# A gated recurrence with a feed-forward layer woven into it: no feed-forward product ahead of the first candidate of a chunk, and no zero-state products in the very first step

## The chip, the cores and the metric

The kernel runs on one core of one Trainium2 chip. The metric is the time of one execution in microseconds (us), lower is better. Engines are named as in the profile: PE is TensorE's matmul side and PEld its weight load, DVE is VectorE, ACT is ScalarE, POOL is GpSimd, SP is SyncE.

## What is computed

x has 2 sequences of 1024 tokens with 256 features. Two layers follow each other, each added to its input:

```
x = x + mixture(x, cond)       # 4 gated experts and 1 shared branch, each 256 -> 1024 -> 256 with gelu
x = x + recurrence(cond, x)    # over the 1024 tokens, state h of 256 per sequence, h starts at zero:
    z = sigmoid(xz[t] + h @ U_z + vz)
    r = sigmoid(xr[t] + h @ U_r + vr)
    hh = tanh(xh[t] + (r * h) @ U + vh)
    h = (1 - z) * h + z * hh
```

xz, xr and xh are products of x (after the first layer) with W_z, W_r and W; the v terms come from cond alone. The gate of each token and expert is found once in the set-up. The recurrence can't be run in parallel over tokens: each step needs the state of the one before.

## The kernel before, in words

**Chunks and steps.** The 1024 steps are 16 chunks c of 64 steps t. One step s = 64 c + t is one pass of the chain PE, ACT, DVE:

1. Reset gate (R): 12 small products (float16 weights, state split into a high and a low part) add h @ U_r to the PSUM bank `r_ps`, in which the input term already lies. Then ACT takes the tanh, and DVE makes p = r * h (`p_cur`, L633) and its low part `p_low` (L646).
2. Update gate (Z): 8 products after those of R (12 in the first step of a chunk, where the shared form of `recur_two` can't be used). DVE collects `z_sum` (L641, or L639 for t = 0), ACT takes its tanh, DVE makes the two halves of `blend` (L654, L656).
3. Candidate (C): 12 products with p once DVE has it, ACT's tanh, and DVE's scan (L662) makes the new state. `h_low` (L665) and `h_high16` (L666) follow, then two operations that the chain does not need at once: `half_h` (L667) and the output `out_feat` (L672).

The semaphore `preact` counts finished gate sums (three a step); ACT waits for it ahead of the tanh of R and C, DVE ahead of `z_sum`. Every engine works its queue in program order, so what stands ahead of an instruction delays it.

**Side work.** While PE would wait inside a step, it computes the first layer for the next chunk. There are two windows in a step: window 0 lies after the Z products and ahead of the C products, window 1 after the C products and ahead of the next step's R products. The work is a list of 165 units, in the order of `units`: 40 tiles of hidden features, each with two `UP` products (float32, 128 columns, two records each in the trace), ACT's gelu, a scaling by the expert's gate on POOL (L288; tiles of the shared branch have none), and two `DOWN` products three tiles later; 2 `BIAS` units; and one `IDLE` unit for each of the first three tiles, a product without use, 256 columns long in window 0 and 384 in window 1 (`IDLE_FILL`). `SIDE[t, w]` says which units go into which window, and `places` how many: 1 in window 0, 2 in window 1 (one less where a finished block of 16 output steps is transposed, `TURNS`). A window with no unit gets that many idle products instead, and so does every window of chunk 15, which has no next chunk. Ahead of the C products comes one more short idle product (`idle_beside_y`, L690).

**Waits of the side work.** The first `UP` of tile i waits for the gelu of tile i - 2, since the two tiles share a PSUM bank (`if n >= 2: pe.wait_ge(gelu_done, n - 1)`, L738). ACT takes the gelu of a tile in the step t + w, where (t, w) is the window of its second `UP` (`GELU_STEP`), and there behind the candidate's tanh. Two other things are placed from the lists: the seeds of the candidate's bank for the next chunk (`c_seeds`, on DVE at the end of a step without a gelu), and the residual add of step 57 (`RESIDUAL_STEP`, L603), which waits for the last `DOWN`. The input products (`PROJECT`) follow from step 58.

**Start.** Chunk 0 of the first layer is computed before the recurrence. Then come two residual adds on DVE, 12 input products (`project(0, g, m, k)`, L774, g in the order R, Z, C) and step 0. The state is zero there, but all its products are issued.

Of the kernel before, what the change touches and what calls it, by code (L numbers as in the profile page):

```python
# [15 lines left out]
P = 128  # L16
# [23 lines left out]
def moe_gru_kernel(nc, x, cond, gate_w, gate_b, time_w, time_b, ew1, eb1, ew2, eb2, sw1, sb1, sw2, sb2,  # L40
# [4 lines left out]
    KC = D // P  # L45
    CT = TOKENS
    CH = T // CT
    COLS = CT * B
# [38 lines left out]
    UP, DOWN, BIAS, TURN, PROJECT, IDLE = "up", "down", "bias", "turn", "project", "idle"  # L87
    SIDE = {(t, w): [] for t in range(CT) for w in range(2)}
    TURNS = [(t, 1) for t in range(1, CT, STEPS)]
    places = lambda t, w: 1 + w - ((t, w) in TURNS)  # L90
    units = []
    for i in range(BR * HT + LAG):
        if i < BR * HT:
# [35 lines left out]
    with ctx:  # L129
        def sb(name, shape, dt=F32):  # L130
            return ctx.enter_context(nc.sbuf_tensor(name, shape, dt))

        def pb(name):
            return ctx.enter_context(nc.psum_tensor(name, [P, RANK], F32))

        def sem(name):
            return ctx.enter_context(nc.semaphore(name))

        x_rows = sb("x_rows", [P, XT, B, D])
        feat = sb("feat", [P, KC, T * B])  # L140
# [12 lines left out]
        wx = sb("wx", [P, GATES, KC, D])  # L153
# [51 lines left out]
        gate_ps = [pb("r_ps"), pb("z_ps"), pb("c_ps")]  # L205
# [59 lines left out]
        preact = sem("preact")  # L265
# [416 lines left out]
        def _(pe):  # L682
            mm = pe.matmul

            def idle(columns, bank=0, start=False):
                mm(up_ps[bank][:, IDLE_AT:IDLE_AT + columns], ident16[:, :], keep_warm[:, 0:columns],
                   start=start, stop=True, skip_group_check=True)
# [7 lines left out]
            for i in range(XT):  # L695
# [4 lines left out]
                for k in range(KC):  # L700
                    for b in range(B):
                        at = (k * B + b) * P
                        last = pe.transpose(turn_ps[i % 2][:, at:at + P], x_rows[:, i, b, k * P:(k + 1) * P],
                                            ident[:, :])
# [11 lines left out]
            for k in range(KC):  # L716
                mm(y_ps[0:B, 64:64 + 2 * E], silu_v[:, k, :], time_w_sb[:, k, :], start=(k == 0), stop=False,
                   skip_group_check=True)
            mm(y_ps[0:B, 64:64 + 2 * E], ones[0:1, 0:B], bias_row[:, 0:2 * E], start=False, stop=True,
               skip_group_check=True)  # L720
# [11 lines left out]
            def up(c, i, k):  # L732
                e, j = TILES[c][i]
                n = TILE0[c] + i
                if k == 0:
                    if c <= 1 and j == 0:
                        pe.wait_ge(up_in[e], 16)
                    if n >= 2:  # L738
                        pe.wait_ge(gelu_done, n - 1)
                last = mm(up_ps[n % 2][:, 0:COLS], up_w[:, e, k, j * P:(j + 1) * P],  # L740
                          feat[:, k, c * COLS:(c + 1) * COLS], start=(k == 0), stop=(k == KC - 1),
                          skip_group_check=True)
                if k == KC - 1:
                    last.then_inc(up_done, 1)
# [26 lines left out]

            def project(c, g, m, k):
                at = (c % 2) * REGION + m * COLS
                mm(gate_ps[g][:, at:at + COLS], wx[:, g, k, m * P:(m + 1) * P], feat[:, k, c * COLS:(c + 1) * COLS],  # L774
                   start=False, stop=False, skip_group_check=True)

            def turn_body(n):
                pe.wait_ge(body_added, n + 1)
                for k in range(KC):
                    last = pe.transpose(rows_ps[:, k * P:(k + 1) * P], out_feat[:, n % 2, k, :], ident[:, :])  # L780
                last.then_inc(turned, 1)

            first_tiles = len(TILES[0])
            for i in range(first_tiles + FIRST_LAG):
# [4 lines left out]
                if i == 4:  # L789
                    pe.wait_ge(agg_made, 1)  # L790
                    for q in range(3):
                        for k in range(KC):
                            mm(y_ps[0:B, 64 + 2 * E:64 + 3 * E], agg[:, q, k, :], gate_w_sb[:, q, k, :], start=False,
                               stop=False, skip_group_check=True)
                    mm(y_ps[0:B, 64 + 2 * E:64 + 3 * E], ones[0:1, 0:B], bias_row[:, 2 * E:3 * E], start=False,
                       stop=True, skip_group_check=True).then_inc(logits_made, 1)
# [5 lines left out]
                if i == FIRST_LAG:  # L802
                    pe.wait_ge(spread_made, 1)
                    mm(y_ps[:, 0:BR * B], ones[0:B, :], spread[:, :, :].rearrange("q e b -> q (e b)"),
                       start=True, stop=True, skip_group_check=True)
                    mm(y_ps[0:BR, 16:16 + B], picked[:, :], ident[0:B, 0:B], start=False, stop=True,
                       skip_group_check=True).then_inc(weights_shared, 1)
# [6 lines left out]
                if i == FIRST_LAG + 8:  # L814
# [3 lines left out]
                    for g in range(GATES):  # L818
                        last = mm(gate_ps[g][:, :], keep_warm[:, 0:P], keep_warm[:, :], start=True, stop=True,
                                  skip_group_check=True)  # L820
# [5 lines left out]
            for k in range(KC):  # L826
                pe.wait_ge(feat_ready, k + 1)
                for g in range(GATES):
                    for m in range(KC):
                        project(0, g, m, k)  # L830
            pe.wait_ge(u_split, GATES)

            HIGH_PRODUCTS = [(m, k, w) for m in range(KC) for k in range(KC) for w in (u_high, u_mid)]
# [3 lines left out]
            def load(g, product):  # L837
                m, k, w = product
                pe.ldweights(w[:, g, k, m * P:(m + 1) * P])  # L839
# [36 lines left out]
            def side(c, t, window):  # L876
                for what, *of in SIDE[t, window]:
                    if what == TURN:
                        n = c * BODIES + t // STEPS
                        if n > 0:  # L880

                            pe.wait_ge(blended, (c * CT + t + 1) * BLEND_STEP + 2)
                            if n > 1:
                                pe.wait_ge(turned_copied, n - 1)
                            turn_body(n - 1)
                    elif what == IDLE:
                        if c < CH - 1:

                            idle(IDLE_FILL[window], (TILE0[c + 1] + of[0]) % 2)
                    elif c < CH - 1:  # L890
                        i, k = of[0], of[1]
                        if what == UP:
                            up(c + 1, i, k)
                        elif what == DOWN:
                            down(c + 1, i, k)
                        elif what == BIAS:
                            output_bias(c + 1, k)
                        else:
                            g, m, k = of
                            if m == 0 and k == 0:  # L900
                                pe.wait_ge(feat_ready, (c + 2) * KC)
                                pe.wait_ge(seeded, (c + 2) * GATES * KC)
                            if g == Z and k == 0:

                                pe.wait_ge(part_ready, (c * CT + t + 1) * PARTS_STEP + Z_CLEAR)
                            project(c + 1, g, m, k)

                real = 0 if c == CH - 1 else sum(what != TURN for what, *_ in SIDE[t, window])
                turning = (t, window) in TURNS
                if real == 0 or c == CH - 1:  # L910
                    for _ in range(1 + window - turning):
                        idle(IDLE_FILL[window])

            for s in range(T):
                c, t = divmod(s, CT)
                parts = s * PARTS_STEP
                load(R, HIGH_PRODUCTS[0])
                pe.wait_ge(part_ready, parts + H_HIGH)
                recur(s, R, False, HIGH_PRODUCTS[0], loaded=True)
                for product in HIGH_PRODUCTS[1:]:  # L920
                    recur(s, R, False, product)
                load(R, LOW_PRODUCTS[0])
                pe.wait_ge(part_ready, parts + H_LOW)
                recur(s, R, True, LOW_PRODUCTS[0], loaded=True)
                for product in LOW_PRODUCTS[1:]:
                    last = recur(s, R, True, product, product is LOW_PRODUCTS[-1])
                last.then_inc(preact, 1)
                for product in MID_PRODUCTS:
                    recur(s, Z, False, product)
                if t == 0:  # L930
                    for product in LOW_PRODUCTS:
                        recur(s, Z, False, product)
                    for product in LOW_PRODUCTS:
                        last = recur(s, Z, True, product, product is LOW_PRODUCTS[-1])
                else:
                    pe.wait_ge(part_ready, parts + H_HIGH16)
                    for product in LOW_PRODUCTS:
                        last = recur_two(s, product, product is LOW_PRODUCTS[-1])
                last.then_inc(preact, 1)
                side(c, t, 0)  # L940
                if t != RESIDUAL_STEP:
                    idle_beside_y(IDLE_SHORT)
                load(C, HIGH_PRODUCTS[0])
                pe.wait_ge(part_ready, parts + PARTS_STEP + P_HIGH)
                recur(s, C, False, HIGH_PRODUCTS[0], loaded=True)
                for product in HIGH_PRODUCTS[1:]:
                    recur(s, C, False, product)
                load(C, LOW_PRODUCTS[0])
                pe.wait_ge(part_ready, parts + PARTS_STEP + P_LOW)
                recur(s, C, True, LOW_PRODUCTS[0], loaded=True)  # L950
                for product in LOW_PRODUCTS[1:]:
                    last = recur(s, C, True, product, product is LOW_PRODUCTS[-1])
                last.then_inc(preact, 1)
                side(c, t, 1)
# [30 lines left out]
```

## Time and profile before

| | |
|---|---|
| median of 3 runs | 1881.32 us (1879.59, 1881.32, 1881.68) |
| profiled execution | 1878.24 us, span in the trace 1876.4 us |
| busy share of the span | PE 98%, PEld 91%, DVE 78%, ACT 38%, POOL 11% |
| mean granted clock of TensorE | 0.999 of full speed |
| chain that ended last | PE 94%, DVE 2%, ACT 2%, issue 1% |

The busy share is the time with an instruction of the engine in flight, so PE at 98% is not PE at its peak: overlapped products and idle products count too. The chain that ended last is followed back through the releases of semaphores; where an engine worked at something else while it waited, the chain stays on that engine.

### The profile page before, as it was taken

How to read it: one execution, taken by the hardware profiler on the slowest of the kernel's cores; microseconds unless marked ns; L12 is line 12 of the kernel's file. 1: busy time of each engine (PE TensorE's matmuls, PEld its weight loads, DVE VectorE, ACT ScalarE, POOL GpSimd, SP SyncE). 2: the span in 40 equal slices, each digit the busy share in tenths (PEclk: the TensorE clock that was granted, in tenths of full speed). 3: DMA queues.
4: the chain of work that ended last, by engine and by line, in shares of the span. 5: the costliest groups of instructions: out<-in, count | busy, mean ns of one | idle time of the engine just before them, and what ended most of it. 6: DMA issues, size and time to landing. Idle time of an engine off the chain costs nothing.

```text
span 1876.4 us, 101766 instructions
## 1 busy us (share of the span) xinstructions
PE 1844.4 (98%) x39969; PEld 1703.9 (91%) x39970; DVE 1454.8 (78%) x11505; ACT 713.4 (38%) x3785; POOL 199.4 (11%) x515
## 2 busy tenths in 40 slices
PE   8999999999999999999999999999999999999998
PEld 8998999989899998999989999899999989999766
DVE  5787878778787787877878787787877878788776
ACT  4333433434333343433434344343433434334322
POOL 0110101101020110101101011110101101011000
PEclk9999999999999999999999999999999999999999
DMA  9000000000000000000000000000000000000000
GB/s 321 4 4 5 5 4 5 5 4 5 5 5 5 4 5 5 4 5 5 4 5 5 4 5 5 4 5 5 4 5 5 4 5 5 5 5 4 5 5 4
DMA packets 16926, 23.62 MB, mean 13 GB/s; under 512 B 3585, under 2 KB 15160, under 8 KB 16445
## 3 DMA queue, kind: packets, MB, share of 16 engines
q1 hardware_dynamic: 15280, 17.05, 2.6%
q8 instruction: 312, 5.11, 1.1%
q14 instruction: 170, 1.38, 0.2%
q10 hardware_dynamic: 1164, 0.07, 0.0%
HBM read 15.01 MB, written 2.10 MB: 9 GB/s over the span
## 4 chain that ended last, share of the span: by engine, by line
PE 94%; DVE 2%; ACT 2%; issue 1%; ACTq 0%; DVEq 0%
PE up_ps L740 20%; PE y_ps L758 20%; PE r_ps L863 13%; PE c_ps L863 13%; PE r_ps L842 6%; PE z_ps L863 6%; PE c_ps L842 5%; PE z_ps L872 4%; ACT rc_tanh_ps L408 2%; PE y_ps L690 2%; DVE h_cur L662 1%; PE c_ps L774 1%; PE z_ps L774 1%; DVE p_cur L633 1%; PE r_ps L774 1%
## 5 line engine op out<-in xcount | busy, mean ns | idle before, releaser
L740 PE MATMUL up_ps<-feat,up_w 128*128 128x128 f32 x2528 | 519.2, 302 | 0.2
L758 PE MATMUL y_ps<-hidden,down_w 128*128 128x128 f32 x2528 | 515.4, 301 | 0.0
L839 PEld LDWEIGHTS <-u_high 128*128 128x128 f16 x4096 | 398.2, 97 | 20.7
L408 ACT ACTIVATE rc_tanh_ps<-r_ps 128x4 f32<-128x4 f32 x1024 | 161.8, 158 | 574.5 <-PE r_ps L863 574.4
L740 PEld LDWEIGHTS up_ps<-feat,up_w 128*128 128x128 f32 x2528 | 362.3, 190 | 1.2 <-ACT hidden L397 0.9
L758 PEld LDWEIGHTS y_ps<-hidden,down_w 128*128 128x128 f32 x2528 | 360.4, 190 | 0.0
L863 PEld LDWEIGHTS r_ps<-h_cur,u_mid 128*128 128x128 f16 x4096 | 252.1, 96 | 113.6 <-issue 46.6
L863 PE MATMUL c_ps<-p_cur,u_mid 128*128 128x40 bf16 (+10 forms) x4096 | 337.4, 179 | 0.0
L863 PE MATMUL r_ps<-h_cur,u_mid 128*128 128x20 bf16 (+5 forms) x4096 | 336.4, 178 | 0.0
L662 DVE TENSOR_TENSOR_SCAN h_cur<-rc_tanh_ps,blend 128x8 f32<-128x8 f32 x1024 | 178.0, 174 | 165.5 <-ACT rc_tanh_ps L408 165.4
L288 POOL TENSOR_TENSOR hidden<-hidden,expert_w 128x128 f32<-128x128 f32 (+3 forms) x416 | 163.9, 394 | 1339.0 <-ACT hidden L397 1339.0
L408 ACT ACTIVATE z_tanh_ps<-z_sum 128x4 f32<-128x4 f32 x1024 | 181.6, 177 | 309.4 <-DVE z_sum L641 304.0
L863 PE MATMUL c_ps<-p_cur,u_high 128*128 128x40 bf16 (+6 forms) x3072 | 285.5, 179 | 0.0
L863 PE MATMUL r_ps<-h_cur,u_high 128*128 128x20 bf16 (+3 forms) x3072 | 285.0, 178 | 0.0
L633 DVE SCALAR_TENSOR_TENSOR p_cur<-rc_tanh_ps,h_cur 128x4 f32<-128x4 f32 x1024 | 166.2, 162 | 138.2 <-ACT rc_tanh_ps L408 126.8
L667 DVE TENSOR_SCALAR half_h<-h_cur 128x4 f32<-128x4 f32 x1024 | 271.9, 266 | 0.0
L863 PEld LDWEIGHTS c_ps<-p_cur,u_mid 128*128 128x128 f16 x4096 | 252.3, 96 | 20.9 <-issue 20.8
L863 PE MATMUL z_ps<-h_cur,u_mid 128*128 128x20 bf16 (+5 forms) x4096 | 259.4, 178 | 0.0
L408 ACT ACTIVATE rc_tanh_ps<-c_ps 128x4 f32<-128x4 f32 x1024 | 161.8, 158 | 252.2 <-PE c_ps L863 252.2
L872 PE MATMUL z_ps<-h_two,u_high 128*128 128x20 f16 x4032 | 240.9, 169 | 0.0
L397 ACT ACTIVATE hidden<-up_ps,small_cols 128x128 f32<-128x128 f32 x632 | 231.6, 367 | 14.5 <-PE up_ps L740 13.2
L672 DVE SCALAR_TENSOR_TENSOR out_feat<-h_cur,h_unscale,feat 128x4 f32<-128x4 f32 x1024 | 223.2, 218 | 0.0
(154 smaller groups left out, 4059.0 us busy)
## 6 DMA issues: line engine op xcount, KB each, us to landing
up_w<-in_L_cond_ew SPq DMA_DIRECT2D x4, 1024.0 KB, 9.3
down_w<-in_L_cond_ew SPq DMA_DIRECT2D x4, 1024.0 KB, 10.4
x_rows<-in_x SPq DMA_DIRECT2D x8, 256.0 KB, 4.6
out<-out_rows SPq DMA_DIRECT2D x128, 16.0 KB, 1.8
up_w<-in_L_cond_sw SPq DMA_DIRECT2D x1, 1024.0 KB, 12.7
down_w<-in_L_cond_sw SPq DMA_DIRECT2D x1, 1024.0 KB, 13.4
cf<-in_L_cond_C_r SPq DMA_DIRECT2D x1, 256.0 KB, 9.6
cf<-in_L_cond_C_z SPq DMA_DIRECT2D x1, 256.0 KB, 9.4
```

What stands on the lines that cost most here:

```text
L397: act.activation(hidden[:, n % TILES_HELD, :], up_ps[n % 2][:, 0:COLS], ACT.Gelu_apprx_tanh, bias=small_cols[:, at:at + 1]).then_inc(gelu_ ...
L408: act.activation((tanh_r, tanh_z, c_now)[g].rearrange("p (m b) -> p m b", b=B), before_tanh, ACT.Tanh, scale=0.5 / GAIN).then_inc(act_done, 1)
L633: dve.scalar_tensor_tensor(p_cur[:, :, 0:B], sq(tanh_r), 1.0, sq(h_now), ALU.add, ALU.mult).then_inc(part_ready, 1)
L662: dve.tensor_tensor_scan(h_cur[:, 0, :], cand, blend[:, :], 0.0, ALU.mult, ALU.add).then_inc(part_ready, 1)
L667: dve.tensor_scalar(half_h[:, :], h_now, -0.5, None, ALU.mult).then_inc(blended, 1)
L672: last = dve.scalar_tensor_tensor(out_feat[:, body % 2, :, row * B:(row + 1) * B], sq(h_now), h_unscale[:, :], feat[:, :, s * B:(s + 1) * ...
L740: last = mm(up_ps[n % 2][:, 0:COLS], up_w[:, e, k, j * P:(j + 1) * P], feat[:, k, c * COLS:(c + 1) * COLS], start=(k == 0), stop=(k == KC ...
L758: last = mm(y_ps[:, m * COLS:(m + 1) * COLS], down_w[:, e, j, m * P:(m + 1) * P], hidden[:, n % TILES_HELD, :], start=False, stop=(m == KC ...
L839: pe.ldweights(w[:, g, k, m * P:(m + 1) * P])
L842: return pe.add_instruction(mybir.InstMatmult(name=nc.get_next_instruction_name(), engine=mybir.EngineType.PE, ins=[pe.lower_ap(moving), p ...
L863: return mm(gate_ps[g][:, at:at + width], w[:, g, k, m * P:(m + 1) * P], moving, start=False, stop=last_of_sum, skip_group_check=True)
L872: return mm(gate_ps[Z][:, at:at + width], w[:, Z, k, m * P:(m + 1) * P], h_two[:, 0:width // B, k * B:(k + 1) * B], start=False, stop=last ...
```

## The change

Three edits. The first takes the one place of window (0, 0) away, so that all 165 units move on by one place and each chunk's first step has an idle product of 256 columns in its window 0. The second and third go together: in step 0 of the whole run no R, Z or C product is issued, only the two windows' side work (without the short idle product), and the last input product of each gate counts `preact` up in their stead. The lists of gelu steps and seeds are derived from `SIDE` and change with it.

```
-    places = lambda t, w: 1 + w - ((t, w) in TURNS)
+    places = lambda t, w: 0 if (t, w) == (0, 0) else 1 + w - ((t, w) in TURNS)
...
             def project(c, g, m, k):
                 at = (c % 2) * REGION + m * COLS
-                mm(gate_ps[g][:, at:at + COLS], wx[:, g, k, m * P:(m + 1) * P], feat[:, k, c * COLS:(c + 1) * COLS],
-                   start=False, stop=False, skip_group_check=True)
+                return mm(gate_ps[g][:, at:at + COLS], wx[:, g, k, m * P:(m + 1) * P],
+                          feat[:, k, c * COLS:(c + 1) * COLS], start=False, stop=False, skip_group_check=True)
...
                 for g in range(GATES):
                     for m in range(KC):
-                        project(0, g, m, k)
+                        last = project(0, g, m, k)
+                    if k == KC - 1:
+
+                        last.then_inc(preact, 1)
...
             for s in range(T):
                 c, t = divmod(s, CT)
                 parts = s * PARTS_STEP
+                if s == 0:
+
+                    side(c, t, 0)
+                    side(c, t, 1)
+                    continue
                 load(R, HIGH_PRODUCTS[0])
```

The lists that follow from it, worked out from the code (U is UP, D is DOWN, I is IDLE, B is BIAS, each with its tile and half; a bar parts window 0 from window 1):

```
step   before                          gelu    after                           gelu
0      U0.0 | I0 U0.1                          (idle) | U0.0 I0
1      U1.0 | I1 TURN                  0       U0.1 | U1.0 TURN                0
2      U1.1 | U2.0 I2                  1       I1 | U1.1 U2.0
3      U2.1 | U3.0 U3.1                2       I2 | U2.1 U3.0                  1
4      B0 | B1 D0.0                    3       U3.1 | B0 B1                    2, 3
5      D0.1 | U4.0 U4.1                        D0.0 | D0.1 U4.0
56     D39.1 | (idle)                          D39.0 | D39.1
seeds of the candidate's bank ahead of steps 24 and 28, after the change ahead of 38 and 42;
residual add at step 57 in both
```

## Rows read from the trace of the kernel before

**Rows 1.** Timeline, DVE: scans around two chunk starts (start us, us, engine, line, operation).
```profile
165.76 0.17 DVE L662 TENSOR_TENSOR_SCAN h_cur<-rc_tanh_ps,blend 128x8 f32<-128x8 f32 x1 [0.17 <-ACT rc_tanh_ps L408]
...
167.60 0.17 DVE L662 TENSOR_TENSOR_SCAN h_cur<-rc_tanh_ps,blend 128x8 f32<-128x8 f32 x1 [0.21 <-ACT rc_tanh_ps L408]
...
169.38 0.17 DVE L662 TENSOR_TENSOR_SCAN h_cur<-rc_tanh_ps,blend 128x8 f32<-128x8 f32 x1 [0.17 <-ACT rc_tanh_ps L408]
...
1758.27 0.17 DVE L662 TENSOR_TENSOR_SCAN h_cur<-rc_tanh_ps,blend 128x8 f32<-128x8 f32 x1 [0.17 <-ACT rc_tanh_ps L408]
...
1760.05 0.17 DVE L662 TENSOR_TENSOR_SCAN h_cur<-rc_tanh_ps,blend 128x8 f32<-128x8 f32 x1
```

**Rows 2.** Timeline, PEld and PE: window 0 of chunk 1's first step.
```profile
166.56 0.30 PEld L740 LDWEIGHTS up_ps<-feat,up_w 128*128 128x128 f32 x2
...
166.89 0.21 PE L690 MATMUL y_ps<-keep_warm,ident 128*128 128x96 bf16 x1
```

**Rows 3.** Timeline: input products and the very first step, three engines.
```profile
51.41 0.61 PE L774 MATMUL z_ps<-feat,wx 128*128 128x128 f32 x4
...
51.86 0.61 PE L774 MATMUL c_ps<-feat,wx 128*128 128x128 f32 x4
...
52.81 0.24 PE L863 MATMUL z_ps<-h_two,u_high 128*128 128x20 f16 x4
...
53.57 0.15 DVE L656 SCALAR_TENSOR_TENSOR blend<-z_tanh_ps,half_h 128x4 f32<-128x4 f32 x1
...
53.74 0.16 ACT L408 ACTIVATE rc_tanh_ps<-c_ps 128x4 f32<-128x4 f32 x1 [0.28 <-PE c_ps L863]
...
53.93 0.17 DVE L662 TENSOR_TENSOR_SCAN h_cur<-rc_tanh_ps,blend 128x8 f32<-128x8 f32 x1 [0.20 <-ACT rc_tanh_ps L408]
```

**Rows 4.** Timeline, ACT and PE: chunk 1, gelu of step 3, first product of step 4.
```profile
172.80 0.37 ACT L397 ACTIVATE hidden<-up_ps,small_cols 128x128 f32<-128x128 f32 x1
...
173.15 0.18 PE L842 MATMUL r_ps<-h_cur,u_high 128*128 128x20 bf16 x1
```

**Rows 5.** Timeline, ACT and PEld, before the recurrence: a gelu waited for, two gelus running.
```profile
17.82 0.37 ACT L397 ACTIVATE hidden<-up_ps,small_cols 128x128 f32<-128x128 f32 x1 [0.77 <-PE up_ps L740]
...
18.24 0.19 PEld L740 LDWEIGHTS up_ps<-feat,up_w 128*128 128x128 f32 x1 [0.20 <-ACT hidden L397]
...
21.46 0.63 ACT L397 ACTIVATE hidden<-up_ps,small_cols 128x128 f32<-128x128 f32 x2
```

**Rows 6.** Timeline, POOL and DVE: one scaling (chunk 1, step 2), two running (chunk 4, step 12).
```profile
169.70 0.40 POOL L288 TENSOR_TENSOR hidden<-hidden,expert_w 128x128 f32<-128x128 f32 x1 [38.72 <-ACT hidden L397]
...
170.27 0.16 DVE L633 SCALAR_TENSOR_TENSOR p_cur<-rc_tanh_ps,h_cur 128x4 f32<-128x4 f32 x1
...
529.51 0.26 POOL L288 TENSOR_TENSOR hidden<-hidden,expert_w 128x42 f32<-128x42 f32 x1 [1.37 <-ACT hidden L397]
...
529.55 0.24 DVE L667 TENSOR_SCALAR half_h<-h_cur 128x4 f32<-128x4 f32 x1
...
529.71 0.37 DVE L672 SCALAR_TENSOR_TENSOR out_feat<-h_cur,h_unscale,feat 128x4 f32<-128x4 f32 x1
...
529.73 0.33 POOL L288 TENSOR_TENSOR hidden<-hidden,nothing 128x86 f32<-128x86 f32 x1
```

**Rows 7.** Timeline, PE and DVE: chunk 1, window 1 of step 55 and the first residual add.
```profile
264.87 0.69 PE L758 MATMUL y_ps<-hidden,down_w 128*128 128x128 f32 x4
...
267.57 0.28 DVE L603 TENSOR_TENSOR feat<-y_ps,feat 128x128 f32<-128x128 f32 x1
```

**Rows 8.** Windows: us, PE, PEld, DVE, ACT, POOL busy (x), granted clock, DMA share, GB/s.
```profile
280.30:283.70 3.40, 3.40 (x58) 3.21 (x55) 1.92 (x17) 0.67 (x5) 0.00 (x0) 0.50 0.00 0
...
1760.00:1870.00 110.00, 99.03 (x2236) 73.89 (x2234) 78.49 (x682) 31.66 (x190) 0.00 (x0) 1.00 0.02 4
```

**Rows 9.** Timeline, DVE: scans of steps 127 and 129, across the start of chunk 2.
```profile
279.44 0.17 DVE L662 TENSOR_TENSOR_SCAN h_cur<-rc_tanh_ps,blend 128x8 f32<-128x8 f32 x1 [0.17 <-ACT rc_tanh_ps L408]
...
284.08 0.17 DVE L662 TENSOR_TENSOR_SCAN h_cur<-rc_tanh_ps,blend 128x8 f32<-128x8 f32 x1 [0.59 <-ACT rc_tanh_ps L408]
```

## The prediction

> **What bounds the kernel now.** I read the busy shares first. PE at 98% looks like the bound, and the chain that ended last agrees, but both count side work and idle products as PE time, so they can't tell a full queue from a filled wait. The timeline can. The scan (L662) ends a step, so the distance of two scans is the step's length. In chunk 1 the scans of steps 63, 64 and 65 start at 165.76, 167.60 and 169.38 [rows 1]: the chunk's first step takes 1.84 us, the next 1.78 us. In chunk 15, whose windows hold nothing but idle products, the first step takes 1760.05 - 1758.27 = 1.78 us too [rows 1]. The 63 steps between scan 64 (167.60) and scan 127 (279.44) average 1.775 us [rows 1, 9], with every mix of UP, DOWN, transposes, seeds and residual adds in them, so a step with float32 units is no longer than one with idle products. What sets its length is the chain from product to tanh to vector operation and back; side work is free as long as it leaves PE, ACT and DVE at the moment when the chain wants them. So the question for each moved unit is what is late behind it.
>
> **The change part by part.**
>
> *The first step of a chunk.* There the Z gate has 12 products instead of 8. The UP unit behind them begins its weight load at 166.56, and the short idle product starts only at 166.89 [rows 2], 0.33 us for one unit, so the candidate's products come late. With an idle product there, as in chunk 15, the step takes 1.78 instead of 1.84 us [rows 1]. I take 0.07 us, since the starts are rounded and the difference lies between 0.05 and 0.08. Chunks 1 to 14 gain it (15 has it already, 0 is counted next): 14 x 0.07 = **-1.0 us**, bounds -0.7 and -1.1.
>
> *The very first step.* The last input products of Z and C end at 51.41 + 0.61 = 52.02 and 51.86 + 0.61 = 52.47 [rows 3]. From then on only ACT and DVE work. Through Z: before, the Z products end at 52.81 + 0.24 = 53.05 and `blend` at 53.57 + 0.15 = 53.72 [rows 3], 0.67 us later, so `blend` is ready at 52.69. Through C: the tanh starts 0.05 us after the products (the release in rows 5), at 52.52, and the scan 53.93 - 53.74 = 0.19 us after the tanh's start [rows 3], at 52.71. Both meet; I take 52.72. The scan moves from 53.93 to 52.72, **-1.2 us**. PE is ready just in time: the input products follow each other at 51.86 - 51.41 = 0.45 us for four records [rows 3], so PE is free for the windows at 52.31; 640 idle columns at 2.4 GHz are 0.27 us and a unit 0.33 us [rows 2], which makes 52.91, and the scan ends at 52.72 + 0.17 = 52.89 [rows 3]. Bounds: -1.0 if PE's windows end last, -1.25.
>
> *A wait in step 3.* Before, the first UP of tile 3 stands in window 1 of step 3 and the gelu of tile 1, for which it waits, in step 2. After the change the UP is still in window 1 of step 3, but the second UP of tile 1 has moved from window (2, 0) to (2, 1), so the gelu of tile 1 moves to step 3, behind that step's candidate tanh. Of all 40 tiles it is the only pair that falls into one step, once in each of chunks 0 to 14. The time of a gelu in step 3 is in the trace: it runs from 172.80 to 173.17, and the next R product comes at 173.15 [rows 4]. PE is released 0.05 us behind a gelu (17.82 + 0.37 = 18.19, weight load at 18.24) [rows 5], at 173.22, and what follows the unit starts 0.33 us after its weight load [rows 2], at 173.55. The R products of step 4 are late by 173.55 - 173.15 = 0.40 us, and nothing but the state's chain stands behind them: they are the chain. 15 x 0.40 = **+6.0 us**. Lower bound: 0.30 a chunk (4.5) if the weight load slips ahead of the wait; upper 0.45 (6.7).
>
> *Two gelus in step 4.* The gelus of tiles 2 and 3 now both stand in step 4. Two running take 0.63 us together [rows 5]; from the usual start, 172.80 [rows 4], they would end at 173.43. The next scan-to-`p_cur` distance of 0.89 us (below) and the 0.19 us from a tanh to the DVE operation behind it put ACT's next tanh at about 173.6, so ACT costs nothing. But both tiles belong to an expert, and POOL scales them one after the other. The first scaling starts 169.70 - 169.38 = 0.32 us behind the scan and takes 0.40 us [rows 1, 6]. Running scalings overlap by 0.04 us (529.51 + 0.26 against 529.73) [rows 6], so the second lasts from 0.68 to 1.08 us behind the scan of step 4. In chunk 4, step 12, a scaling in two pieces shows what DVE does meanwhile: `half_h` ends at 529.79, 0.02 us after the first piece, and `out_feat` at 530.08, 0.02 us after the second [rows 6]. They are held until POOL is done. There the pieces were short enough. With two full ones `out_feat` ends at 1.10, and the operation behind it in DVE's queue, `p_cur`, starts 0.08 us before that (as 529.71 against 529.79) [rows 6], at 1.02 instead of 170.27 - 169.38 = 0.89 [rows 1, 6]. The candidate's products wait for `p_cur`. So 0.13 us a chunk, 15 x 0.13 = **+1.9 us**. Bounds: 0 if `out_feat` gets in between the two scalings; 15 x 0.21 = 3.2 without that overlap.
>
> *What costs nothing.* The last DOWN moves from window 0 to window 1 of step 56. Two such units in step 55 end at 264.87 + 0.69 = 265.56; a step of 1.78 later that is 267.34, and the residual add starts at 267.57 [rows 7]. Cover 0.23 us; gone, each us would go to DVE and the next `p_cur`. The candidate's seeds move to other steps of the same kind, with no gelu in front. All other units only change windows, among steps that average 1.775 us whatever they hold [rows 1, 9]. The added counts on `preact` queue behind nothing.
>
> **Sum:** -1.0 - 1.2 + 6.0 + 1.9 = **+5.7 us**. On the profiled execution 1878.24 gives 1883.9. The median of the runs shown is 3.1 us above that execution, 0.16%, for reasons that no trace here shows; part of it may be the clock (below). Added to the median: 1881.3 + 5.7 = 1887.0 us, 0.30% slower.
>
> **The clock.** From 280.30 to 283.70 the granted clock is 0.50 of full speed (1.2 of 2.4 GHz) [rows 8]. Before it PE had gone through steps 62 and 63 with idle products alone, and stood at the start of chunk 2. From scan 127 to scan 129 it took 284.08 - 279.44 = 4.64 us [rows 9], against 1.84 + 1.78 = 3.62: one such stretch costs 1.0 us. But chunk 15, idle products throughout and PE busy 99.03 of 110 us, ran at clock 1.00 [rows 8]. The change leaves PE less to do at just these places, in the first window and beside the wait in step 3. The Trainium skill (TensorE: Matmul & The Clock Gate, "What's actually happening") says that activity releases the throttle and its lack brings it back, which speaks against thinning PE out at a chunk's start. By that rule alone a fall at every one of the 15 chunk starts would add 14 x 1.0 = 14 us; by the rows of chunk 15 nothing. I put 0 into the sum, nearer to 109 us of rows than to one event, and up to 3 us into the range.
>
> **Rivals.**
>
> *A, both waits (the forecast):* +5.7, 1887.0.
>
> *B, the wait in step 3 alone:* `out_feat` slips between the two scalings. For it: DVE issues it before POOL's second starts. Against: in chunk 4 it was issued before the second piece too (529.71 against 529.73) and still held. +3.8, 1885.1.
>
> *C, not slower:* the wait in step 3 costs nothing, because the gelu is done when PE comes to it. It decides at the point where PE must start the unit to be out by 173.15, that is 172.82 in the times of rows 4; the gelu would have to end by 172.77 and it ends at 173.17. Only if ACT took it ahead of the candidate's tanh would it hold; the queue says otherwise. Then -2.2 + 1.9 = -0.3 (1881.0), and -2.2 (1879.1) if the scalings cost nothing either.
>
> *D, the clock falls more often:* three to fourteen more stretches at 1.0 us over A, 1890 to 1901. For it the one event and its place; against it chunk 15.
>
> That the first edit doesn't do what it says (the candidate still late because of the idle product put in the unit's place) is excluded by chunk 15, where just this product stands there.
>
> **How the numbers follow.** Chances: A 0.63, B 0.17, C 0.08, D 0.12. What a measurement of this kernel can tell from no change is about 0.2%, 3.8 us. A is slower by more than that over nearly all of its bounds (its lower end 4.5 + 1.9 - 2.2 = 4.2); B lies on the line and is split; C is the same; D is slower. That gives slower 0.80, same 0.17, faster 0.03, the last for a median that moves with the clock. The range goes from B with a little less wait, 1884.0, to A with three more stretches at half clock, 1889.8.
>
> **What would show it.** Scans at each chunk start 1.78 us apart; the first scan near 52.7; in the list of waits PEld L740 waiting for ACT's gelu (L397) 15 times inside the recurrence, about 0.3 us each, and the R products behind it 0.4 us late; in step 5 `out_feat` held to 1.10 us behind the scan and `p_cur` at 1.02; a page otherwise unchanged. Wrong would be: no such wait, scans of steps 3 to 6 all at 1.78 us, or a granted clock of 0.50 at many chunk starts.

## The result and the profile after

| | before | changed |
|---|---|---|
| median of 8 runs each, same chip | 1881.07 us | 1886.05 us |
| lowest, highest | 1879.59, 1882.28 | 1885.32, 1890.21 |
| profiled execution, span | 1878.24, 1876.4 us | 1887.49, 1885.7 us |

The ratio is 1.0030, with a 95% interval of 1.0021 to 1.0039: the change makes the kernel slower by 5.0 us. Forecast were 5.7 us, 1887.0 us and a range of 1884.0 to 1889.8. The changed kernel run again on another chip (`e0_changed_again`, below) came out 6.2 us slower.

The busy shares of the changed kernel's page say nothing of it; they are those of before within one point:

```profile
PE 1849.4 (98%) x39918; PEld 1707.2 (91%) x39918; DVE 1449.7 (77%) x11505; ACT 713.0 (38%) x3785; POOL 197.8 (10%) x515
```

The timeline of DVE with the scans alone (start us, us) shows it. These are steps 63 to 70, the counterpart of [rows 1]:

```profile
167.89 0.17 DVE L662 TENSOR_TENSOR_SCAN h_cur<-rc_tanh_ps,blend 128x8 f32<-128x8 f32 x1 [0.17 <-ACT rc_tanh_ps L408]
...
169.67 0.17 DVE L662 TENSOR_TENSOR_SCAN h_cur<-rc_tanh_ps,blend 128x8 f32<-128x8 f32 x1
...
173.22 0.17 DVE L662 TENSOR_TENSOR_SCAN h_cur<-rc_tanh_ps,blend 128x8 f32<-128x8 f32 x1 [0.17 <-ACT rc_tanh_ps L408]
...
175.00 0.17 DVE L662 TENSOR_TENSOR_SCAN h_cur<-rc_tanh_ps,blend 128x8 f32<-128x8 f32 x1 [0.18 <-ACT rc_tanh_ps L408]
...
177.17 0.17 DVE L662 TENSOR_TENSOR_SCAN h_cur<-rc_tanh_ps,blend 128x8 f32<-128x8 f32 x1 [0.17 <-ACT rc_tanh_ps L408]
...
179.06 0.17 DVE L662 TENSOR_TENSOR_SCAN h_cur<-rc_tanh_ps,blend 128x8 f32<-128x8 f32 x1 [0.18 <-ACT rc_tanh_ps L408]
...
180.84 0.17 DVE L662 TENSOR_TENSOR_SCAN h_cur<-rc_tanh_ps,blend 128x8 f32<-128x8 f32 x1 [0.17 <-ACT rc_tanh_ps L408]
```

The first step of the chunk now takes 169.67 - 167.89 = 1.78 us instead of 1.84. Steps 1 to 3 are plain. The scan of step 4 comes 177.17 - 175.00 = 2.17 us behind that of step 3, the scan of step 5 another 179.06 - 177.17 = 1.89 us later, and from there on steps are plain again. Chunks 0 to 14 all show the same: step 4 between 2.172 and 2.177 us, step 5 between 1.886 and 1.891, plain steps 1.776.

**The wait in step 3.** Timeline of ACT, PEld and PE of the changed kernel, and under it the row of its waits (us in total, times, longest):

```profile
174.88 0.37 ACT L397 ACTIVATE hidden<-up_ps,small_cols 128x128 f32<-128x128 f32 x1
...
175.30 0.30 PEld L740 LDWEIGHTS up_ps<-feat,up_w 128*128 128x128 f32 x2 [0.39 <-ACT hidden L397]
175.51 0.10 PEld L842 LDWEIGHTS <-u_high 128*128 128x128 f16 x1
...
175.62 0.18 PE L845 MATMUL r_ps<-h_cur,u_high 128*128 128x20 bf16 x1
```

```profile
PEld up_ps L740 <- ACT hidden L397: 6.4, 18, 0.4
```

The gelu ends at 174.88 + 0.37 = 175.25, the weight load of tile 3's first UP starts 0.05 us later, and the next step's R products 0.32 us behind that. Of the eighteen waits for a gelu three lie in the set-up ([rows 5] show such a one) and fifteen in the recurrence. The weight loads stood idle 0.39 us ahead of this unit (the prediction had said about 0.3).

**The held operation in step 5.** The same step on ACT, POOL and DVE; x2 are two instructions running:

```profile
177.05 0.62 ACT L397 ACTIVATE hidden<-up_ps,small_cols 128x128 f32<-128x128 f32 x2
...
177.50 0.76 POOL L288 TENSOR_TENSOR hidden<-hidden,expert_w 128x128 f32<-128x128 f32 x2 [1.77 <-ACT hidden L397]
...
177.53 0.38 DVE L667 TENSOR_SCALAR half_h<-h_cur 128x4 f32<-128x4 f32 x1
177.84 0.44 DVE L672 SCALAR_TENSOR_TENSOR out_feat<-h_cur,h_unscale,feat 128x4 f32<-128x4 f32 x1
...
178.19 0.15 DVE L633 SCALAR_TENSOR_TENSOR p_cur<-rc_tanh_ps,h_cur 128x4 f32<-128x4 f32 x1
```

The two scalings end at 178.26. `out_feat` takes 0.44 us instead of 0.21 and ends at 178.28; `p_cur` starts 178.19 - 177.17 = 1.02 us behind the scan, against 0.89 in [rows 6].

**The very first step.** Timeline of PE and DVE, the counterpart of [rows 3]:

```profile
54.54 0.61 PE L774 MATMUL c_ps<-feat,wx 128*128 128x128 f32 x4
...
55.23 0.15 DVE L656 SCALAR_TENSOR_TENSOR blend<-z_tanh_ps,half_h 128x4 f32<-128x4 f32 x1
...
55.48 0.17 DVE L662 TENSOR_TENSOR_SCAN h_cur<-rc_tanh_ps,blend 128x8 f32<-128x8 f32 x1
```

From the last candidate input products to the scan it is 55.48 - 54.54 = 0.94 us, before 53.93 - 51.86 = 2.07: 1.13 us gained. That all of it starts later than before comes from the set-up, ahead of the changed code. Windows of the changed kernel's set-up (columns as in [rows 8], the granted clock third from last) show

```profile
7.00:21.00 14.00, 13.32 (x111) 10.60 (x109) 7.68 (x27) 10.59 (x21) 0.00 (x0) 1.00 1.06 379
21.00:31.00 10.00, 10.00 (x62) 9.72 (x62) 7.37 (x38) 3.45 (x9) 0.39 (x1) 0.66 1.06 401
31.00:49.00 18.00, 18.00 (x161) 17.73 (x160) 10.49 (x32) 7.83 (x21) 0.00 (x0) 1.00 0.66 241
...
1424.80:1428.20 3.40, 3.40 (x59) 3.05 (x55) 1.91 (x17) 0.69 (x6) 0.00 (x0) 0.50 0.00 0
```

a stretch at 1.2 GHz between 21 and 31 us, in code that the change does not touch and though PE had been busy 13.32 of the 14 us before it, and one more stretch at half clock at a chunk start, as before had one. `e8_wait_alone_in_before` and `e9_pair_alone_in_before`, which hold none of the three edits, have such a stretch in the set-up too. So the difference of the two spans, 9.3 us, is not the change's price. It is made up of: set-up later by 2.7 (first input product at 52.24, before 49.56), first step -1.1, 14 chunk starts -1.0, waits 15 x 0.398 = +6.0, held operations 15 x 0.111 = +1.7, stretches at half clock -0.1, and 1024 plain steps longer by 1.1 ns each, +1.1. That is 9.3. The change's own parts sum to +5.6 (+5.5 with unrounded terms), against 5.0 measured over the medians.

### The profile page after: what moved, and what is told of

Its sections match the earlier page's. It is cut to its first block, busy times and chain, and to the rows that moved or that the text cites. A ratio compares the mean times of both kernels' runs of the same rounds, so it can differ in the third digit from the quotient of the medians.

```text
span 1885.7 us, 101663 instructions
## 1 busy us (share of the span) xinstructions
PE 1849.4 (98%) x39918; PEld 1707.2 (91%) x39918; DVE 1449.7 (77%) x11505; ACT 713.0 (38%) x3785; POOL 197.8 (10%) x515
## 4 chain that ended last, share of the span: by engine, by line
PE 92%; DVE 3%; ACT 3%; issue 1%; ACTq 0%; DVEq 0%
PE up_ps L740 19%; PE y_ps L758 19%; PE r_ps L866 13%; PE c_ps L866 13%; PE r_ps L845 6%; PE z_ps L866 6%; PE c_ps L845 5%; PE z_ps L875 4%; ACT rc_tanh_ps L408 2%; PE y_ps L690 2%; DVE h_cur L662 1%; DVE p_cur L633 1%; PE c_ps L774 1%; PE z_ps L774 1%; PE r_ps L774 1%
## 5 line engine op out<-in xcount | busy, mean ns | idle before, releaser
L866 PE MATMUL c_ps<-p_cur,u_mid 128*128 128x40 bf16 x4092 | 337.3, 180 | 0.0
L866 PE MATMUL r_ps<-h_cur,u_mid 128*128 128x20 bf16 x4092 | 335.9, 178 | 0.0
L866 PE MATMUL c_ps<-p_cur,u_high 128*128 128x40 bf16 x3069 | 285.6, 179 | 0.0
L866 PE MATMUL r_ps<-h_cur,u_high 128*128 128x20 bf16 x3069 | 284.5, 178 | 0.0
L667 DVE TENSOR_SCALAR half_h<-h_cur 128x4 f32<-128x4 f32 x1024 | 265.9, 260 | 0.0
L866 PE MATMUL z_ps<-h_cur,u_mid 128*128 128x20 bf16 x4092 | 259.1, 178 | 0.0
```

Of the source, the lines that this page charges most:

```text
L667: dve.tensor_scalar(half_h[:, :], h_now, -0.5, None, ALU.mult).then_inc(blended, 1)
L866: return mm(gate_ps[g][:, at:at + width], w[:, g, k, m * P:(m + 1) * P], moving, start=False, stop=last_of_sum, skip_group_check=True)
```

## The experiments

The kernels ran in three groups, each on one chip with its own runs of the kernel before: `e1` to `e4` in the first, `e5` to `e7` and `e0` in the second, `e8` to `e10` in the third. Times are differences of medians within a group.

**Each half of the change alone.** The first has only the new `places`, the second all but that line.

```
e1_lists_only:       - places = lambda t, w: 1 + w - ((t, w) in TURNS)
                     + places = lambda t, w: 0 if (t, w) == (0, 0) else 1 + w - ((t, w) in TURNS)
e2_first_step_only:  the edits of project, of its last call and of s == 0
```

> Theory of the two waits: all of the loss comes with the lists. Against the kernel before: 15 waits in step 3 (+0.40 us each, the scan of step 4 at 2.17 to 2.18 us behind that of step 3), 15 held operations in step 5 (+0.11 each, as in the profile of the changed kernel), -0.07 us for each of 15 first steps: +6.0 + 1.7 - 1.0 = +6.6 us, 0.35% slower, 1.5 us slower than the whole change. Rival, the loss is the clock's (falls at chunk starts, whatever the lists do in steps 3 to 5): scans of steps 4 and 5 at 1.78 us, granted clock 0.50 at several chunk starts.

> Theory: the scan of step 0 comes 1.1 to 1.2 us earlier behind the last input product, everything else as before: -1.1 us, 0.06% faster, not to be told from no change by its time but to be read from the profile (0.94 us from the start of the last candidate input products to the first scan, against 2.07 before). Rival, the saved products thin TensorE out and the clock or the first window's unit takes the gain back: first scan less than 0.5 us earlier.

Measured: the lists alone 1885.48 against 1879.15 us, +6.3, ratio 1.0032 (1.0019 to 1.0044). The first step alone 1878.19, -1.0, ratio 0.9993 (0.9984 to 1.0002), which its time can't tell from no change. The timeline of the second (PE, DVE) does: 54.63 - 53.69 = 0.94 us to the first scan.

```profile
53.69 0.61 PE L774 MATMUL c_ps<-feat,wx 128*128 128x128 f32 x4
54.63 0.17 DVE L662 TENSOR_TENSOR_SCAN h_cur<-rc_tanh_ps,blend 128x8 f32<-128x8 f32 x1
```

The profile of the lists alone had no stretch at half clock inside the recurrence at all, nor in the set-up, and its span was 6 us longer than that of before all the same (1882.5 against 1876.4): scans of steps 3 to 6 at 174.49, 176.66, 178.54 and 180.32. The loss is the lists', and not the clock's.

**The cause taken away.** Three edits of the changed kernel.

```
e3_idle_unit_dropped:   - *([(IDLE, i, 0)] if i < LAG else [])
                        + *([(IDLE, i, 0)] if 0 < i < LAG else [])
e4_gelu3_a_step_later:  - GELU_STEP.setdefault(t + w, []).append(i)
                        + GELU_STEP.setdefault(t + w + (i == 3), []).append(i)
e5_gelu1_in_step2:      + GELU_STEP.setdefault(t + w - (i == 1), []).append(i)
```

> The whole change, but the idle unit of tile 0 is dropped from the list, so that from step 1 on each window holds what it held before the change. Theory of the two waits: no wait for a gelu inside the recurrence, no step with two gelus, all steps at 1.775 us: -1.0 - 1.1 = -2.1 us against before, 7 to 8 us less than the changed kernel. Rival, the cost is in the thinner first window (clock): then the time stays near that of the changed kernel, 1886, or at least above before.

> The whole change, with the gelu of tile 3 in step 5 instead of beside that of tile 2 in step 4; the wait in step 3 stays. Theory: scan of step 5 at 1.775 us instead of 1.887, scan of step 4 still 2.17: -15 x 0.11 = -1.7 us against the changed kernel, +3.3 against before. Rival, the 0.11 us come from something else behind the wait in step 3 (a late product, the order of the units): step 5 stays at 1.89.

> The whole change, with the gelu of tile 1 put behind the candidate's tanh of step 2, though its second UP product is in window 1 of that step: ACT waits there for the product, PE no longer waits in step 3. The two gelus in step 4 stay. Theory: scan of step 4 at 1.775 us, scan of step 5 still 1.887: -6.0 us against the changed kernel, -0.4 against before. Rivals: ACT's wait in step 2 delays the next reset tanh (step 3 longer than 1.78 us; the gelu would have to end later than the R products of step 3); or the two costs hang together and step 5 falls to 1.775 as well, because the wait ahead of it is gone.

Measured: with the idle unit dropped 1877.30 against 1879.15 us, -1.85, ratio 0.9989 (0.9980 to 0.9998): the one version below before with its whole interval, though only by half of the 3.8 us that the prediction took as what a time can tell. With the gelu of tile 3 moved 1882.70, +3.6, ratio 1.0018 (1.0009 to 1.0027). With the gelu of tile 1 moved (second group) 1879.93 against 1879.77, +0.2, ratio 0.9999 (0.9990 to 1.0008). Timeline of DVE, scans of steps 3 to 5, with the gelu of tile 3 moved:

```profile
173.49 0.17 DVE L662 TENSOR_TENSOR_SCAN h_cur<-rc_tanh_ps,blend 128x8 f32<-128x8 f32 x1 [0.18 <-ACT rc_tanh_ps L408]
175.66 0.17 DVE L662 TENSOR_TENSOR_SCAN h_cur<-rc_tanh_ps,blend 128x8 f32<-128x8 f32 x1 [0.18 <-ACT rc_tanh_ps L408]
177.44 0.17 DVE L662 TENSOR_TENSOR_SCAN h_cur<-rc_tanh_ps,blend 128x8 f32<-128x8 f32 x1 [0.17 <-ACT rc_tanh_ps L408]
```

and of steps 2 to 5 with the gelu of tile 1 moved:

```profile
172.33 0.17 DVE L662 TENSOR_TENSOR_SCAN h_cur<-rc_tanh_ps,blend 128x8 f32<-128x8 f32 x1 [0.17 <-ACT rc_tanh_ps L408]
174.12 0.17 DVE L662 TENSOR_TENSOR_SCAN h_cur<-rc_tanh_ps,blend 128x8 f32<-128x8 f32 x1 [0.18 <-ACT rc_tanh_ps L408]
175.90 0.17 DVE L662 TENSOR_TENSOR_SCAN h_cur<-rc_tanh_ps,blend 128x8 f32<-128x8 f32 x1 [0.18 <-ACT rc_tanh_ps L408]
177.79 0.17 DVE L662 TENSOR_TENSOR_SCAN h_cur<-rc_tanh_ps,blend 128x8 f32<-128x8 f32 x1 [0.17 <-ACT rc_tanh_ps L408]
```

The first keeps 2.17 for step 4 and has 1.78 for step 5; the second has 1.78 for step 4 and keeps 1.89 for step 5. The two costs don't depend on each other. The rival of a delayed reset tanh came true in a small way: step 3 takes 174.12 - 172.33 = 1.79 us, 0.02 us more than plain, and 1.93 us in chunk 4 alone; why it is more there is open. In chunks 1 to 14 ACT has, at this place, also the copy of a transposed block:

```profile
172.53 0.37 ACT L397 ACTIVATE hidden<-up_ps,small_cols 128x128 f32<-128x128 f32 x1 [0.23 <-PE up_ps L740]
172.79 0.36 ACT L415 ACTIVATE out_rows<-z_tanh_ps 32x256 f32<-32x256 f32 x1
173.06 0.15 ACT L408 ACTIVATE rc_tanh_ps<-r_ps 128x4 f32<-128x4 f32 x1
```

The reset tanh at 173.06 has no idle time in front of it: ACT is just full.

**ACT or POOL, both moves together, and the changed kernel again.** The rest of the second group.

```
e6_scaling3_later:    pool.wait_ge(gelu_done, n + 1)
                      + if i == 3:
                      +     pool.wait_ge(part_ready, ((c - 1) * CT + 6) * PARTS_STEP + P_LOW)
e7_both_gelus_moved:  + GELU_STEP.setdefault(t + w - (i == 1) + (i == 3), []).append(i)
e0_changed_again:     the changed kernel, unchanged
```

> The whole change, but POOL scales tile 3 only when the low part of step 5's p is written; both gelus stay in step 4. It parts ACT from POOL as the cause of the 0.11 us in step 5. POOL holding DVE: scan of step 5 at 1.775 us, the time 1.7 us below the changed kernel (the same as with the gelu moved). ACT's second gelu as the cause: step 5 stays at 1.89. The later scaling may hold other operations of step 5 with two SBUF operands, none of which stands on the chain.

> The whole change with both moves of gelus (tile 1 to step 2, tile 3 to step 5), so that the lists of products stay as changed. Theory: all steps at 1.775 us, -2.1 us against before, as with the idle unit dropped. If the products' places themselves cost something (three thinner windows 0 in steps 0, 2 and 3), this one is slower than the kernel with the idle unit dropped, by what their steps and their stretches at half clock show.

> The changed kernel once more, on the same chip as the three others of this call: +5.0 us against before as measured, steps 4 and 5 of chunks 0 to 14 at 2.17 and 1.89 us. It shows how much of the 9.3 us between the two profiled spans is the state of the clock in the set-up (2.7 us in the profile of the changed kernel) and not the change: first input product at 49.6 us if the set-up runs at full clock, later by up to 3 us if not.

Measured against 1879.77 us: the later scaling 1884.35, +4.6, ratio 1.0021 (1.0013 to 1.0030); both gelus moved 1877.78, -2.0, ratio 0.9992 (0.9983 to 1.0001); the changed kernel again 1885.94, +6.2, ratio 1.0032 (1.0019 to 1.0045). The later scaling is 1.6 us below the changed kernel of its group, 15 x 0.11 = 1.7 expected. Its timelines of ACT, DVE and POOL, step 5 of chunk 1 (two lines were added, so `p_cur` is L635 here and the scan L664):

```profile
176.92 0.63 ACT L399 ACTIVATE hidden<-up_ps,small_cols 128x128 f32<-128x128 f32 x2
...
177.04 0.17 DVE L664 TENSOR_TENSOR_SCAN h_cur<-rc_tanh_ps,blend 128x8 f32<-128x8 f32 x1 [0.17 <-ACT rc_tanh_ps L410]
...
177.70 0.21 DVE L674 SCALAR_TENSOR_TENSOR out_feat<-h_cur,h_unscale,feat 128x4 f32<-128x4 f32 x1
...
177.93 0.16 DVE L635 SCALAR_TENSOR_TENSOR p_cur<-rc_tanh_ps,h_cur 128x4 f32<-128x4 f32 x1
...
178.44 0.40 POOL L288 TENSOR_TENSOR hidden<-hidden,expert_w 128x128 f32<-128x128 f32 x1 [0.67 <-DVE z_ps L652]
...
178.81 0.17 DVE L664 TENSOR_TENSOR_SCAN h_cur<-rc_tanh_ps,blend 128x8 f32<-128x8 f32 x1 [0.17 <-ACT rc_tanh_ps L410]
```

Both gelus still run back to back, `out_feat` takes 0.21 us again, `p_cur` is 0.89 behind the scan, and the step takes 1.77. It is POOL's second scaling that held DVE, and not ACT's second gelu.

With both gelus moved and the changed lists of products kept, the time is 2.0 us below before, with the idle unit dropped 1.85; the medians alone can't part the two. The steps can: steps 0 to 6 are plain in chunks 0 to 14 but for step 3, which takes 1.79 us in chunks 1 to 14 (1.93 in chunk 4) as with the gelu of tile 1 moved alone. So the new places of the products cost nothing that the scans show. The changed kernel again has steps 4 and 5 at 2.17 and 1.89 us. Its first input product comes at 52.17 us, with 6.8 us of its set-up at half clock, so nothing shows how early it comes when the set-up runs at full clock.

**Each cost put into the kernel before.** The third group.

```
e8_wait_alone_in_before:  + GELU_STEP.setdefault(t + w + (i in (1, 2, 3)), []).append(i)
e9_pair_alone_in_before:  + GELU_STEP.setdefault(t + w + (i == 2), []).append(i)
```

> The kernel before, none of the three edits in it, but ACT takes the gelus of tiles 1, 2 and 3 a step later (steps 3, 4 and 5 instead of 2, 3 and 4). The products stay where they were and no step has two gelus, so only the wait ahead of the first UP of tile 3 is put in. Theory: scan of step 4 at 2.17 us in chunks 0 to 14, all other steps unchanged, +6.0 us, 0.32% slower. Rival, the wait only costs where the lists are thinned as in the change: the step stays at 1.775 us.

> The kernel before with the gelu of tile 2 moved from step 3 to step 4, beside that of tile 3; nothing else. Theory: two scalings in a row on POOL, scan of step 5 at 1.89 us in chunks 0 to 14, no wait of PE for a gelu, +1.7 us, 0.09%, to be read from the profile. Rival, the pair costs only behind a late step 4: step 5 stays at 1.775 us.

Measured against 1881.04 us: the wait 1890.43, +9.4, ratio 1.0052 (1.0035 to 1.0069); the pair 1882.90, +1.9, ratio 1.0010 (1.0001 to 1.0020), with step 5 at 1.886 to 1.891 us in chunks 0 to 14 (scans at 176.11 and 178.00). The pair is as forecast. The wait is there, but half as dear again: DVE's scans of steps 3 and 4 and PEld's row between them,

```profile
176.01 0.17 DVE L662 TENSOR_TENSOR_SCAN h_cur<-rc_tanh_ps,blend 128x8 f32<-128x8 f32 x1 [0.17 <-ACT rc_tanh_ps L408]
178.40 0.17 DVE L662 TENSOR_TENSOR_SCAN h_cur<-rc_tanh_ps,blend 128x8 f32<-128x8 f32 x1 [0.17 <-ACT rc_tanh_ps L408]
```

```profile
176.30 0.52 PEld L740 LDWEIGHTS up_ps<-feat,up_w 128*128 128x128 f32 x4 [0.61 <-ACT hidden L397]
176.74 0.10 PEld L839 LDWEIGHTS <-u_high 128*128 128x128 f16 x1
```

give 2.40 us for step 4. I had counted one unit behind the wait, as in the changed kernel. Before the change window 1 of step 3 holds both UPs of tile 3, and both wait (x4 records, two units): the R weights are loaded 0.44 us behind the first UP's, in the changed kernel 0.21. By the scans that is 2.40 - 1.78 = 0.62 us instead of 0.40, times 15 is 9.3.

**The clock.** The kernel with the idle unit dropped, and without idle products in the empty windows of steps 62, 63 and 0 of chunks 0 to 14; nothing of the computation is missing.

```
- if real == 0 or c == CH - 1:
+ if (real == 0 or c == CH - 1) and (c == CH - 1 or t not in (62, 63, 0)):
```

> The kernel with the idle unit dropped, and besides without any idle product in the unit-less windows of steps 62, 63 and 0 of chunks 0 to 14 (the short one ahead of the candidate stays). It asks what the idle product does that the change puts into window (0, 0). If the clock depends on how busy TensorE is, the granted clock falls to half at most of the 15 chunk starts, at 0.9 to 1.0 us each as in the two profiles: +9 to +15 us over the kernel with the idle unit dropped. If it doesn't, steps at 1.775 us and the same time as that kernel.

Measured 1900.68 against 1881.04 us, +19.6, ratio 1.0106 (1.0091 to 1.0121). Windows of it around the starts of chunks 1, 2 and 3:

```profile
150.00:164.50 14.50, 13.50 (x309) 12.05 (x306) 10.57 (x91) 4.10 (x25) 0.00 (x0) 1.00 0.02 4
164.50:174.80 10.30, 9.69 (x165) 8.71 (x165) 6.09 (x50) 3.08 (x18) 0.80 (x2) 0.50 0.02 5
...
280.60:290.80 10.20, 9.55 (x166) 8.52 (x164) 6.17 (x50) 2.96 (x16) 0.80 (x2) 0.50 0.01 3
...
400.10:403.40 3.30, 3.30 (x56) 2.88 (x52) 2.15 (x17) 1.11 (x6) 0.40 (x1) 0.50 0.02 5
```

The clock is at 1.2 GHz at each of the starts of chunks 1 to 15, for 3.4 to 10.2 us. From first to last scan it took 1841.1 us against 1816.8 with the idle products, 1.6 us for each chunk start. By the medians against before it is 21.5 us more than the kernel with the idle unit dropped, where 9 to 15 were expected: I had multiplied the 0.9 to 1.0 of one stretch of 3.4 us; seven of the fifteen stretches are that short, three last 6.8 and five 10.2 us.

So the mechanism of rival D exists. Seven idle products were taken away together, and which of them matter is not shown, but for this: at the start of chunk 15 the one of step 0 was kept, and the clock fell all the same. The change does not bring it about: inside the recurrence, the profiles of the changed kernel and of the eight experiments of the first two groups show 0 to 2 stretches at half clock; before shows 1, and so does `e9_pair_alone_in_before`. They lie late in a chunk, at a chunk's start, or in chunk 15.

## Why the prediction was right

- *First step of a chunk, 0.07 us each.* Right: 1.775 us in chunks 1 to 14 (the one of chunk 12 had its stretch at half clock). A step with an idle product in window 0 was to be read off chunk 15 before anything was changed.
- *Very first step, 1.2 us.* Right in kind, 1.13 in the profile: `blend` ended 0.67 us behind the Z products and the candidate's tanh began at 55.19, both as forecast, but the scan came 0.10 us behind `blend` (55.38 to 55.48) and not at once, as I had put it.
- *The wait, 0.40 us a chunk.* Right: 0.398. Experiments with the wait taken out by two different edits (-6.0 us against the changed kernel of the same group, and the idle unit dropped, which takes away the pair too) and put in alone show it as the cause.
- *Two gelus, 0.13 us a chunk.* Right in mechanism, down to the start of `p_cur` at 1.02 us. The size was 0.111: from `p_cur` to the next scan it took 0.87 us instead of 0.88, so 0.01 to 0.02 us came back. Two operations with all operands in SBUF were held beside the scalings: `half_h` took 0.38 us instead of 0.16, `out_feat` 0.44 instead of 0.21. In `e6_scaling3_later` the second half of `blend`, which reads PSUM too, ran beside the second scaling from 178.49 on in its usual 0.15 us. Two gelus in one step don't matter.
- *Nothing else.* Right: all other steps of the changed kernel are under 1.79 us, but for those in its stretch at half clock and four of chunk 15 (2, 18, 34 and 50) at 1.82, which take 1.83 before the change. That chunk 15 has them went unsaid in the prediction; they don't move its sum.
- *The sum.* Forecast +5.7, parts in the profile +5.5: the first step gave 0.1 us less than forecast and the held operations cost 0.2 less. The medians, 5.0 and 6.2 us, can't tell these apart. Two figures of the prediction are slightly off and nothing hangs on them: three stretches over A make 1890.0 and not 1889.8, and the rows of chunk 15 cover 110 us and not 109.
- *Rival C* would have needed the gelu ahead of the tanh; *rival B* fell with the held `out_feat`; *rival D*'s 1.0 us is right for a stretch of 3.4 us, but stretches can last three times as long; it did not happen here.
- *Level.* I went by the median of the three runs shown. That it lay 3.1 us above the profiled execution would fit the set-up: the profiled execution of before had its whole set-up at full clock and the earliest first input product of all thirteen profiles, 49.56 us, where the others have 49.9 to 52.3. It is not shown for those very runs.

## What to carry to other kernels

When a list of side work is moved by one place, every rule that is derived from the places moves too: go through the list pair by pair for waits that now fall into the step of their own releaser, and for two pieces of work of another engine that now fall into one. Price such a wait by its release and by all that is queued behind it up to the next instruction of the chain: two units cost 0.62 us where one cost 0.40. And ahead of moving anything, look for a stretch that already has the shape of the new one (here chunk 15): it gives the gain, and often it shows a cheaper way, here dropping the idle unit instead of pushing the list.

## What the hardware showed that I had not expected

- The same set-up code ran at full clock in some profiles and partly at half in others, with and without the change. The first input product came at 49.6 to 50.8 us in four profiles at full clock, at 50.8 to 51.4 in four with 3.4 us at half, and at 51.8 to 52.3 in five with 6.8 us at half. So of the 2.7 us between the two profiles compared above about 2 are the clock's, an estimate from the means of these three sets; the rest is open. A single pair of profiles (9.3 us apart) would have overstated the change's 5.6 us by two thirds.
- Taking 7 idle products away around each chunk start (6 at that of chunk 15) cost about 21 us in all, by the differences to before in two groups (+19.6 and -1.85): the clock was at half for up to 10.2 us, into step 3, though first-layer products had come back in step 0.
- Plain steps differ between profiles, 1.7743 to 1.7763 us (mean of all scan distances below 1.79 us), whatever the kernel; over 1024 steps that is up to 2 us. Only differences against runs of the same chip were used for times.
